# A graph network's second node pass: the first product of the update and all that follows it moved one half later than the transposed activations

## What is computed

```python
h = relu(layernorm(x))
x = x + batchnorm(edge_softmax_sum(h, src, dst) + relu(h @ W_res + b_res))      # layer 0
h = relu(layernorm(x))                                                          # "h2"
m = gelu(gelu(concat(h[src], h[dst], edge_attr) @ W_m1 + b_m1) @ W_m2 + b_m2)
boxes = segment_sum(m, dst)
c = gelu(concat(h, boxes) @ W_c1 + b_c1)
out = x + h + gelu(c @ W_c2 + b_c2)                                             # layer 1
```

## Time and profile before

| what | us |
|---|---|
| three runs, median | 1633.65 |
| lowest and highest | 1632.19, 1642.5 |
| the profiled execution | 1630.99 |
| its span, first to last instruction | 1629.2 |
| TensorE busy in the span | 1290.4 |
| VectorE busy | 1234.1 |
| ScalarE busy | 945.8 |

### The profile page before, as it was taken

How to read it: one execution, slowest core, us unless ns; L and a number is a source line. 1 busy time by engine, 2 the same in 40 slices (tenths; PEclk the granted TensorE clock), 3 DMA queues, 4 the chain that set the end, 5 groups by cost and what they waited for, 6 DMA issues and landing times.

```text
span 1629.2 us, 21884 instructions
## 1 busy us (share of the span) xinstructions
PE 1290.4 (79%) x6227; PEld 777.5 (48%) x6227; DVE 1234.1 (76%) x2432; ACT 945.8 (58%) x1647; POOL 1093.4 (67%) x989
## 2 busy tenths in 40 slices
PE   4566665558778778767999989999969999999983
PEld 2233332247666667654545444444444454554431
DVE  8898888488988988866777777777667777777661
ACT  5688786623323323326777777777646676666651
POOL 7788887777777777777776057667735555445355
PEclk8888788757877877878999999999989999999985
DMA  7666675468876543354655467666375454454410
GB/s 211 222 224 195 206 221 199 146 223 294 275 275 221 142 124 115 91 194 139 203 185 192 163 209 230 202 202 201 113 230 151 142 159 133 143 158 130 123 50 16
DMA packets 141969, 287.34 MB, mean 176 GB/s; under 512 B 33104, under 2 KB 50614, under 8 KB 141852
## 3 DMA queue, kind: packets, MB, share of 16 engines
q1 hardware_dynamic: 109532, 255.32, 46.9%
q0 software_dynamic: 32320, 30.62, 8.0%
HBM read 165.47 MB, written 121.80 MB: 176 GB/s over the span
## 4 chain that ended last, share of the span: by engine, by line
PE 47%; DVE 18%; POOL 16%; issue 10%; ACT 6%; DMA 2%; SPq 0%; DVEq 0%; POOLq 0%; ACTq 0%
POOL x_ring L607 8%; POOL gout L607 7%; PE banks L1501 6%; PE banks L1478 6%; PE banks L1525 4%; PE banks L1407 3%; PE banks L1598 3%; PE banks L1596 3%; PE banks L1424 3%; PE banks L1605 3%; PE banks L1511 3%; DVE sums L841 3%; ACT cT L1230 2%; DVE gout L1016 2%; PE banks L1491 2%
## 5 line engine op out<-in xcount | busy, mean ns | idle before, releaser
L607 POOL DMA_INDIRECT agg_ring<-agg_rows,edge_idx x196 | 213.5, 1089 | 161.4 <-DMA edge_agg<-agg_ring 97.5
L611 POOL DMA_INDIRECT out<-agg,put_last x196 | 196.5, 1002 | 184.3 <-DVE agg L1048 129.3
L607 POOL DMA_INDIRECT x_ring<-in_x,edge_idx x200 | 239.2, 1196 | 63.5 <-issue 63.5
L607 POOL DMA_INDIRECT gout<-in_x,edge_idx x192 | 226.2, 1178 | 58.5 <-issue 58.2
L611 POOL DMA_INDIRECT agg_rows<-agg,put_first x196 | 216.9, 1107 | 59.7 <-issue 55.8
L738 DVE TENSOR_REDUCE stat<-sq 128x16 f32<-128x1024 f32 (+1 forms) x98 | 118.7, 1213 | 26.3 <-ACT sq L1093 21.9
L1229 ACT ACTIVATE cT<-banks,packed 96x512 f32<-96x512 f32 (+1 forms) x98 | 66.8, 682 | 107.4 <-PE banks L1501 107.3
L963 DVE TENSOR_TENSOR xc<-banks,xc 128x512 f32<-128x512 f32 (+1 forms) x74 | 51.2, 692 | 92.2 <-PE banks L1525 90.9
L1501 PE MATMUL banks<-hT,packed 64*96 64x512 f32 (+1 forms) x392 | 112.6, 652 | 2.8 <-ACT hT L1222 2.8
L1365 PE MATMUL banks<-ident,xc 128*128 128x128 f32 (+1 forms) x296 | 54.4, 345 | 75.9 <-DVE xc L767 64.9
L1511 PE MATMUL banks<-cT,packed 96*64 96x512 f32 (+1 forms) x392 | 105.5, 616 | 0.4 <-ACT gout L1238 0.4
(11 more groups left out here) (191 smaller groups left out, 3384.8 us busy)
## 6 DMA issues: line engine op xcount, KB each, us to landing
xt<-in_x SPq DMA_DIRECT2D x48, 512.0 KB, 6.1
r_rows<-rT SPq DMA_DIRECT2D x48, 512.0 KB, 7.0
xe<-edge_x SPq DMA_DIRECT2D x96, 256.0 KB, 3.8
agg_rows<-rb SPq DMA_DIRECT2D x48, 512.0 KB
xt<-in_x_t SPq DMA_DIRECT2D x36, 512.0 KB, 5.0
out<-xc SPq DMA_DIRECT2D x36, 512.0 KB, 3.2
edge_r<-rr SPq DMA_DIRECT2D x48, 256.0 KB, 3.8
rT<-r_rows SPq DMA_DIRECT2D x24, 512.0 KB, 5.6
```

The lines of the kernel that those rows point to most:

```text
L607: A.indirect_dma_start(to, None, table[:, :], bass.IndirectOffsetOnAxis(ap=idx, axis=0), bounds_check=limit, oob_is_err=False).then_inc(si ...
L611: A.indirect_dma_start(table[:, :], bass.IndirectOffsetOnAxis(ap=idx, axis=0), rows_of, None, bounds_check=limit, oob_is_err=False).then_i ...
```

## The change

- TensorE: c_product(u - 1), out_product(u - 3), transpose_back(u - 4) where there were u, u - 2, u - 3. The four center_x2 of a pair stand two in half 4i, one each in 4i + 1 and 4i + 2. The waits around bank 6 are shifted with it.
- ScalarE: copy_h2T(u), gelu_out(u - 3), norm_r or square_x2, gelu_c(u - 1). norm_r stands in odd halves, square_x2 in even ones.
- VectorE: the same order, add_out and final_half one half later.
- h2 has a fifth buffer, made of x_ring 0 and 1 (h2_half).
- SP: the rows are stored in two halves of columns, load_r is issued two steps further ahead, load_rows and the stores are in another order.

```diff
+HS = 5
...
-        B_st = slots("final_rows_stored", 4)
+        B_st = slots("final_rows_stored", HS, 32)
...
+        def h2_half(s, b):
+            return x_ring[b][:, :] if s % HS == 4 else h2[s % HS][:, b * HALF:(b + 1) * HALF]
...
             def store_final(s):
-                B_fin.done(sp, s)
-                p = nodes_of(s)
-                sp.dma_start(dense_rows(out, s), h2[s % 4][0:p, :]).then_inc(B_st.of(s), 16)
+                p = nodes_of(s)
+                for b in range(2):
+                    B_fin.part(sp, s, b + 1)
+                    sp.dma_start(dense_rows(out, s)[:, b * HALF:(b + 1) * HALF], h2_half(s, b)[0:p, :])\
+                      .then_inc(B_st.of(s), 16)
...
-            for s in range(4, XS):
+            for s in range(4, XB):
                 load_rows(s)
-            for s in (4, 5):
+            for s in range(4, 8):
                 load_r(s)
             for i in range(PAIRS + 1):
                 a, b = 2 * i, 2 * i + 1
-                for s in (a + 6, b + 6):
-                    if is_step(s):
-                        load_r(s)
...
-                for s in (a - 2, b - 2):
+                if is_step(a - 2):
+                    store_final(a - 2)
+                if i and is_step(a + 6):
+                    load_rows(a + 6)
+                for s in (a + 8, b + 8):
                     if is_step(s):
-                        store_final(s)
-                    if is_step(s + 8):
-                        load_rows(s + 8)
+                        load_r(s)
+                if i and is_step(b + 6):
+                    load_rows(b + 6)
+                if is_step(b - 2):
+                    store_final(b - 2)
...
             def relu_half(u):
                 s, p, c = half_of(u)
-                B_st.done(dve, s - 4)
+                B_st.done(dve, s - HS)
...
             for i in range(PAIRS + 1):
                 a, b, u = 2 * i, 2 * i + 1, 4 * i
-                each((add_out, u - 3), (relu_half, u + 2), (relu_half, u + 3))
+                each((add_out, u - 4), (relu_half, u + 2), (relu_half, u + 3))
                 if is_step(a + 4):
                     add_r(a + 4)
-                each((final_half, u - 3), (add_out, u - 2))
+                each((final_half, u - 4), (add_out, u - 3))
                 if is_step(a + 2):
                     sum_x2(a + 2)
                 if is_step(b + 4):
                     add_r(b + 4)
-                each((final_half, u - 2), (add_out, u - 1))
+                each((final_half, u - 3), (add_out, u - 2))
                 if is_step(b + 2):
                     sum_x2(b + 2)
-                invert_pair(i + 1, lambda: each((final_half, u - 1)))
-                each((add_out, u), (relu_half, u + 4), (final_half, u), (relu_half, u + 5))
+                invert_pair(i + 1, lambda: each((final_half, u - 2)))
+                each((add_out, u - 1), (relu_half, u + 4), (final_half, u - 1), (relu_half, u + 5))
...
-            for u in range(2 * S + 2):
+            for u in range(2 * S + 3):
                 s = u // 2
                 if is_half(u):
                     copy_h2T(u)
-                if u % 4 == 0 and is_step(s + 2):
-                    square_x2(s + 2)
-                if u % 4 == 1 and is_step(s + 3):
-                    square_x2(s + 3)
-                if is_half(u - 2):
-                    gelu_out(u - 2)
-                if is_half(u):
-                    gelu_c(u)
+                if is_half(u - 3):
+                    gelu_out(u - 3)
                 if u < 2:
                     norm_r(u + 4)
-                if u % 4 == 2 and is_step(s + 5):
-                    norm_r(s + 5)
-                if u % 4 == 3 and is_step(s + 6):
+                if u % 2 == 0 and is_step(s + 2):
+                    square_x2(s + 2)
+                if u % 2 == 1 and is_step(s + 6):
                     norm_r(s + 6)
+                if is_half(u - 1):
+                    gelu_c(u - 1)
...
             def transpose_h2(u):
...
-                B_fin.part(pe, (u - 4) // 2, u % 2 + 1)
+                if 0 < u < 5:
+                    pe.wait_ge(B_ht.sem, u)
+                B_fin.part(pe, (u - 5) // 2, (u - 5) % 2 + 1)
...
             def transpose_back(u):
...
-                if is_half(u + 3):
-                    pe.wait_ge(B_ht.sem, u + 4)
+                if is_half(u + 4):
+                    pe.wait_ge(B_ht.sem, u + 5)
...
-            for u in range(2 * S + 3):
+            centers = ((4, 5), (5,), (5,), ())
+            for u in range(2 * S + 4):
                 if is_half(u):
                     transpose_h2(u)
-                if u % 4 < 2:
-                    for k in (u + 4, u + 5) if u % 4 == 0 else (u + 5, u + 6):
-                        if is_half(k):
-                            center_x2(k)
-                if is_half(u - 2):
-                    out_product(u - 2)
                 if is_half(u - 3):
-                    transpose_back(u - 3)
-                if is_half(u):
-                    c_product(u)
+                    out_product(u - 3)
+                for k in centers[u % 4]:
+                    if is_half(u + k):
+                        center_x2(u + k)
+                if is_half(u - 4):
+                    transpose_back(u - 4)
+                if is_half(u - 1):
+                    c_product(u - 1)
```

More of the change, by code:

```diff
@@ L948, in relu_half @@
                 s, p, c = half_of(u)
-                B_st.done(dve, s - 4)
-                relu_scale(rows(h2[s % 4][0:p, c]), rows(W[s % 2][0:p, c]), dstat(3, s, p)[:, (u % 2) * 8:(u % 2) * 8 + 8],
+                B_st.done(dve, s - HS)
+                relu_scale(rows(h2_half(s, u % 2)[0:p, :]), rows(W[s % 2][0:p, c]), dstat(3, s, p)[:, (u % 2) * 8:(u % 2) * 8 + 8],
                            B_h)
@@ L960, in final_half @@
                 s, p, c = half_of(u)
-                here = h2[s % 4][0:p, c]
+                here = h2_half(s, u % 2)[0:p, :]
                 dve.wait_ge(B_bt.sem, u + 1)
@@ L1283, in square_edges @@
                 if g == 0:
-                    B_st.done(act, S - 4)
+                    B_st.done(act, S - 3)
                 A.activation(esq[g % 2][0:p, :], bank(3 + g % 2)[0:p, :], ACT.Square).then_inc(C_sq.sem, 1)
@@ L1490, in transpose_h2 @@
                     c = (4 * b + i) * P
-                    ins = T.transpose(bank(6)[:, i * P:i * P + p], h2[s % 4][0:p, c:c + P], ident[0:p, 0:p])
+                    ins = T.transpose(bank(6)[:, i * P:i * P + p], h2_half(s, b)[0:p, i * P:(i + 1) * P], ident[0:p, 0:p])
                 ins.then_inc(B_t.sem, 1)
```

## The result

The kernel after takes 1692.84 us (median of four runs, 1689.42 to 1698.45), before 1632.92: a ratio of 1.0351, 95% interval 1.0314 to 1.0389, so 60 us slower. I had said 1680, with 1636 to 1704 as the range.

The account below looks back on a forecast made before the run. TensorE was taken to bound the second node pass; 16.46 of work, 2.64 stall and 1.57 clock gave 20.67 us a pair, 454.7 over 22 pairs against 408.9, +45.8, hence 1680 us, range 1636 to 1704.

Parts of the forecast that it names:

- The stall: Second node pass: TensorE waits ahead of T(4i+3) for VectorE's final(4i-2), 2.64 us per pair.
- The chain from the end of C(4i+7) to T: Square, sum, five inversion instructions and final before T(4i+3): 4.26 us, against 1.62 of TensorE's B and c beside it.
- VectorE's wait ahead of the sum: VectorE waits for ScalarE's square ahead of the sum, about 3.4 us once per pair.
- The waits of before: TensorE's waits ahead of B for ScalarE's copy of hT, 0.34 and 1.46 us per pair; forecast nearly gone.
- these 1.87 us per pair: TensorE's waiting within before's 18.33 us pair, beyond 16.46 of work; claimed removable by the change.
- The ring that I drew: Between TensorE and ScalarE: c, gelu, norm, copy, B, c; before put c(u) behind the copy of the same half.
- The clock: TensorE's granted clock falls after the wait: one low stretch per pair, 1.57 us, making 20.67 a pair.
- the 454.7 I had summed: The 22 pairs from T(4) to T(92) after the change, 22 x 20.67 us, against 408.9 before.
- clock holds: Rival: the stall comes but the clock doesn't fall; 19.10 us a pair, 1645 us, chance 0.18.
- faster: Rival: no stall if C(4i+7) to final(4i-2) takes under 1.62 us; 16.46 a pair, 1587 us, chance 0.11.
- SP, buffer and stores: Fifth h2 buffer, stores by halves and SP's order: hidden, cost 0, at most a few us if something came late.
- Fill and drain: Pipeline ends: fill some 3 us less, drain about 2.5 us more; together 0, kept at -4 to +4.

Follow-up runs that it names:

- experiment 1: Kernel after with the four center_x2, square_x2 and norm_r of a pair placed as in before; 1599.66 us, 0.9781 of before.
- 2: Kernel after, centers still spread, VectorE doing add_out(u-1) and final(u-2) before the sum of squares; 1.0039 of before on the slower chip.
- experiment 4: Kernel before with ScalarE's norm_r ahead of gelu_c in the same half; 1595.40 us, 0.9751 of before.
- 9: Kernel of experiment 1 with gelu_c's two activations split around the next copy of hT and norm_r moved into halves with centers; 1589.91 us, 0.9728 of before.
- experiment 3: Kernel after with extra unread products on TensorE where it waits: five, 1.0326 of before on the slower chip; three, 1651.39 us, 1.0114 of before.
- experiment 7: Kernel before with the fifth h2 buffer, stores by halves and SP's new order of loads and stores; 1634.43 us, 0.9991 of before.
- experiment 5: Kernel before with only the centers spread as in after and the square of step 2i+3 one half later; 1650.95 us, 1.0116 of before.
- experiment 6: Kernel after with out_product behind the centers again, centers still spread; 1706.34 us, 1.0445 of before.
- 8: Kernel of experiment 1 with ScalarE's gelu_c moved behind the next copy of hT; 1602.14 us, 0.9806 of before.

## Why the prediction was right, point by point

The number first, since part of its closeness is luck. Between the profiled executions I had 1676.8 and it took 1698.45, 21.7 us more. The medians miss by 13 only, because before's profiled execution lay 2.7 us below its median, which I added, while after's lay 5.6 above. Of the 21.7, 19.3 are in the 22 pairs and the rest outside them.

The stall: right in place (T(4i+3), behind final(4i-2)), in cause and nearly in size. The chain from the end of C(4i+7) to T measured 4.46 us, I had 4.26; the square started 0.20 behind the center's end instead of 0.04, and T 0.15 behind final instead of 0.06. Stall 2.83, forecast 2.64. In the first five pairs it was 3.10 to 3.14; two of the five small instructions of the inversion took longer there (0.39 and 0.26 us in one pair), why is open. VectorE's wait ahead of the sum, forecast at 3.4, was 3.48. Experiments 1 and 2 show the cause from both ends: without the late center, or without VectorE's order, the wait at T(4i+3) is gone (0.73 is left in 2, at T(4i+4)).

The waits of before: right, none is left in the 22 pairs. But "So these 1.87 us per pair can go" puts no price on each part of the change, and experiment 4 shows that 1.12 of it is norm_r's place alone. The ring that I drew (c, gelu, copy, B, c) stands after the change too, and it leaves 0.34 in each half without a center (experiment 1). The cut of gelu_c, with norm_r moved, opens it (9).

The clock: right in kind, too small in size, and this is the term that explains most of the miss. I took one low stretch a pair at 1.57 us. Over the 22 pairs the granted clock was 0.90: 474 x 0.10 = 47 us, 2.2 a pair, since 8 of the 21 low stretches lasted twice as long. In before 0.98 gives 8. The forecast's term was 22 x 1.57 = 35; measured about 47, 12 more. The stall adds 63.8 - 22 x 2.64 = 6. Together that is 18 of the 19 us by which 474.0 exceeds the 454.7 I had summed. The rival "clock holds" (1645) describes what comes out when TensorE is kept at work: experiment 3 with three products gave 1651.

By the Trainium skill ("TensorE: Matmul & The Clock Gate", Why this matters for your kernels) stalls of 2.83 us, as in 17 of the 22 pairs, shouldn't have cost any clock. The trace of after, with a low stretch behind 16 of these 17, and experiment 3, without the gap and without a low stretch behind it, decide against that here.

The rival "faster" fell at the point that I gave it: the chain was 4.46 against a cover of 1.6. Experiment 1 is that rival with the chain moved; it took 1600, and not 1587, for the 0.34 twice a pair.

SP, buffer and stores: right, 0 (experiment 7). Fill and drain: the fill -4.8 (I had -3), T(92) to the last final +2.7 (2.5). The pass behind it took 3.5 us more, which I hadn't counted. TensorE there waits 4.53 us once for VectorE's add_agg, where before waited 1.88, and in both VectorE itself waits for a load (weighted from edge_agg): in the chains that ended last it took 6.52 us from 1202.56 in before, and 9.14 us from 1265.91 in after. That is 2.6 of the 3.5 us. Why the load took longer is open, and no run tests it.

What I passed over: the change also puts out_product ahead of the centers. I used the order of after in the sum (cover B + c), so the number held, but I never priced it. My expectation for experiment 5 took the 2.8 us along without it and was wrong by 48 us; for experiment 6 I then missed the order on ScalarE.

## What to carry to other kernels

When a stage is bound by one engine in a written order, spreading its work evenly is only worth something if the piece that a chain on other engines starts from isn't the one that moves back: count what stands behind that piece on the bound engine against the whole chain, and read every engine's order with it, since they fit in pairs. A stall that recurs every 20 us may cost once as waiting and again through TensorE's clock; here that second cost was about six tenths of the loss. Before pipelining deeper, look for a long instruction that sits inside the ring and could stand outside; here one moved call was worth 37 us, and the deeper pipeline with the same call moved gave no more (33, experiment 1). The fastest kernel, 5 us ahead of the moved call, has the deeper pipeline and the gelu on the ring cut in two; the cut without the deeper pipeline was not run.

## What the runs showed that I had not expected

Two products with 64 output rows each, into the two halves of the partitions, take 1.01 us together; products of the same size into one half took about 0.9 us each (2.79 for three, 4.43 for five). So the pair in out_product overlaps.

The clock fell behind gaps of 1.8 to 2.1 us too (experiment 5, low stretches in 14 of the 22 pairs, 0.94 over them), and stayed at 1.00 over the 22 pairs (369.5 to 381.2 us) where no gap was above 0.5 (experiments 1, 4, 8 and 9). The same gaps don't always do the same: with the same 44 waits of up to 1.46 us, four low stretches begin in the 22 pairs of before's profiled execution and eight in those of experiment 7, which took 415.0 us against 408.9.

The same before took 1632 to 1635 us on two chips and 2046.8 on another, and there the kernels that win 2.2 to 2.5% elsewhere win 0.7 to 0.8%.
